# An attention loop over four chunks of time, with the norm and K product of the next chunk moved ahead of the recurrence and output product of this one

## What is computed

```python
x = x + attn(_layernorm(x))
# attn: xx is x shifted by one position
xk = x * time_mix_k + xx * (1.0 - time_mix_k)
xv = x * time_mix_v + xx * (1.0 - time_mix_v)
xr = x * time_mix_r + xx * (1.0 - time_mix_r)
k = xk @ W_key.T; v = xv @ W_value.T; r = xr @ W_receptance.T
sr = sigmoid(r)
# per channel, over t:  y = (p + e^(u+k) v) / (q + e^(u+k));
#   p = e^w p + e^k v;  q = e^w q + e^k      (w = -exp(time_decay), u = time_first)
out = (sr * y) @ W_output.T
```

## Time and profile before

| | us |
|---|---|
| median of the runs (2932.19 and 2935.12) | 2933.66 |
| the profiled execution, its own time | 2935.05 |
| span of its slowest core, first to last instruction | 2933.5 |
| span of its fastest core | 2923.3 |

### The profile page before, as it was taken

How to read it: one execution, slowest core, us unless ns; L and a number is a source line. 1 busy time by engine, 2 the same in 40 slices (tenths; PEclk the granted TensorE clock), 3 DMA queues, 4 the chain that set the end, 5 groups by cost and what they waited for, 6 DMA issues and landing times.

```text
span 2933.5 us, 21628 instructions; the slowest of 8 cores (2923.3 to 2933.5 us)
## 1 busy us (share of the span) xinstructions
PE 1877.2 (64%) x7648; PEld 785.1 (27%) x7648; DVE 1278.5 (44%) x1772; ACT 326.9 (11%) x551; POOL 67.9 (2%) x88
## 2 busy tenths in 40 slices
PE   3414324324322368878878878878878878888785
PEld 1101101101100123333333333333333333333332
DVE  5456456446455562143433423434434424424433
ACT  0320320210310000000000000010010010010000
POOL 0000000000001000000000000000000000000000
PEclk7757756656655689989989889989889889889897
DMA  6503503403209010021321321321311212213203
GB/s 149 81 0 69 75 0 51 64 0 55 31 0 129 1 24 1 1 36 15 50 36 15 51 36 15 51 36 15 50 24 28 38 27 37 36 17 49 29 1 115
DMA packets 69195, 112.79 MB, mean 38 GB/s; under 512 B 2480, under 2 KB 37312, under 8 KB 68048
## 3 DMA queue, kind: packets, MB, share of 16 engines
q0 software_dynamic: 63856, 94.50, 22.6%
q1 hardware_dynamic: 5232, 16.91, 1.8%
HBM read 197.28 MB, written 8.52 MB: 70 GB/s over the span
## 4 chain that ended last, share of the span: by engine, by line
PE 51%; DVE 9%; issue 2%; ACT 1%; DVEq 0%; DMA 0%; ACTq 0%; POOLq 0%
PE pc L638 18%; PE pc L664 15%; PE pc L652 14%; DVE h L707 4%; DVE sg L706 4%; PE pc L603 2%; PE pc L622 1%; ACT sg L736 1%; PE pc L611 1%; DVE h L677 1%; DVE acc L680 1%; DVE acc L715 0%; DVE h L689 0%; DVEq L36 0%; DMA cb<-comb_dram 0%
## 5 line engine op out<-in xcount | busy, mean ns | idle before, releaser
L638 PE MATMUL pc<-ln2x,wsl 128*128 128x512 bf16 x1920 | 521.6, 439 | 190.9 <-ACT sg L736 189.9
L664 PE MATMUL pc<-h,wsl 128*128 128x512 bf16 x1920 | 461.4, 404 | 101.6 <-DVE h L707 100.6
L706 DVE TENSOR_TENSOR sg<-sg,pc 128x512 f32<-128x512 f32 x240 | 164.9, 687 | 824.6 <-PE pc L652 805.2
L652 PE MATMUL pc<-ln2x,wsl 128*128 128x512 bf16 x1920 | 427.6, 379 | 0.0
L715 DVE TENSOR_TENSOR acc<-acc,pc 128x512 f32<-128x512 f32 x480 | 330.0, 688 | 183.5 <-PE pc L664 144.4
L638 PEld LDWEIGHTS pc<-ln2x,wsl 128*128 128x128 bf16 x1920 | 206.7, 110 | 504.6 <-issue 345.0
L736 ACT ACTIVATE sg<-pc 128x512 f32<-128x512 f32 x240 | 143.3, 597 | 1524.9 <-PE pc L638 1018.4
L338 PE MATMUL pb<-sry,wsla 128*128 128x512 bf16 x256 | 67.8, 435 | 379.7 <-DVE sry L257 379.7
L664 PEld LDWEIGHTS pc<-h,wsl 128*128 128x128 bf16 x1920 | 190.2, 102 | 372.8 <-issue 192.5
L652 PEld LDWEIGHTS pc<-ln2x,wsl 128*128 128x128 bf16 x1920 | 187.6, 98 | 230.2
L338 PE MATMUL pb<-mx,wsla 128*128 128x512 bf16 x512 | 127.3, 415 | 126.6 <-DVE mx L218 100.3
(11 more groups left out here) (118 smaller groups left out, 903.5 us busy)
## 6 DMA issues: line engine op xcount, KB each, us to landing
wsl<-gw POOLq DMA_DIRECT2D x15, 1024.0 KB, 11.5
wsl<-uw POOLq DMA_DIRECT2D x15, 1024.0 KB, 11.2
wsl<-dw POOLq DMA_DIRECT2D x15, 1024.0 KB, 12.0
acc<-x SPq DMA_DIRECT2D x4, 2048.0 KB, 24.4
wsla<-wk POOLq DMA_DIRECT2D x4, 2048.0 KB, 17.5
wsla<-wv POOLq DMA_DIRECT2D x4, 2048.0 KB, 19.0
wsla<-wr POOLq DMA_DIRECT2D x4, 2048.0 KB, 17.3
wsla<-wo POOLq DMA_DIRECT2D x4, 2048.0 KB, 17.7
```

What stands on the lines that cost most here:

```text
L638: inst = t.matmul(pc4[tc][:], slot_ap(3 * e)[:, kc, ocI * 128:(ocI + 1) * 128], ln2x[:, kc, 2 + tc * 512: 2 + (tc + 1) * 512], start=(kc = ...
L652: inst = t.matmul(pc4[4 + tc][:], slot_ap(3 * e + 1)[:, kc, ocI * 128:(ocI + 1) * 128], ln2x[:, kc, 2 + tc * 512: 2 + (tc + 1) * 512], sta ...
L664: inst = t.matmul(pc4[(oc % 2) * 4 + tc][:], slot_ap(3 * e + 2)[:, kcI, oc * 128:(oc + 1) * 128], h[:, kcI, tc * 512:(tc + 1) * 512], star ...
L706: VS.do(lambda sl=sl, tc=tc: v.tensor_tensor(sl[:], sl[:], pc4[4 + tc][:], OP.mult))
```

## The change

The norm, the difference and the K and V mixes of a chunk become a function `prework`. It is called once for chunk 0 ahead of the loop, and then for chunk `s_ + 1` inside chunk `s_`, between the evacuation of V and the recurrence. The statistics and the K product of chunk `s_ + 1` go with it: on TensorE they stand between R and O of chunk `s_`. O of chunk `s_` is added to `acc` in chunk `s_ + 1`, between the R mix and the evacuation of V. ScalarE makes the reciprocal root of chunk `s_ + 1` after the sigmoid of chunk `s_`. GpSimd's and SyncE's programs are not changed. No instruction is added or left out on any engine.

The diff, cut (the body of `prework` is the old code with `sp` for `s_`):

```diff
 @blk.vector
-                for s_ in range(NSC):
...
+                def prework(sp):
...
                     VS.do(lambda: v.tensor_tensor(xsq[:], ln1x[:, :, 1:], ln1x[:, :, 0:SCW], OP.subtract))
+                    if sp >= 1:
+                        v.wait_ge(s_pe, MS(f"t:MAT{4 * (sp - 1) + 2}"))
...
+                prework(0)
+                for s_ in range(NSC):
                     v.wait_ge(s_pe, MS(f"t:MAT{4 * s_ + 0}"))
+                    if s_ >= 1:
+                        v.wait_ge(s_sc, MS(f"s:ea{s_ - 1}_3"))
...
                     VS.ms[f"v:mixr{s_}"] = VS.v
+                    if s_ >= 1:
+                        psl = slice((s_ - 1) * SCW, s_ * SCW)
+                        v.wait_ge(s_pe, MS(f"t:MAT{4 * (s_ - 1) + 3}"))
+                        for od in range(CC):
+                            VS.do(lambda od=od, psl=psl: v.tensor_tensor(
+                                acc[:, od, psl], acc[:, od, psl], pb[od][:], OP.add))
+                        VS.ms[f"v:accev{s_ - 1}"] = VS.v
                     v.wait_ge(s_pe, MS(f"t:MAT{4 * s_ + 1}"))
...
                     VS.ms[f"v:vevac{s_}"] = VS.v
+                    if s_ + 1 < NSC:
+                        prework(s_ + 1)
                     for l in range(4):
...
 @blk.scalar
+                emit_rstd(0)
                 for s_ in range(NSC):
-                    s.wait_ge(s_dv, MS(f"v:var1_{s_}"))
-                    SS.do(lambda: s.activation(pb[2][:], pb[2][:], AF.Ln))
-                    SS.do(lambda: s.activation(pb[2][:], pb[2][:], AF.Exp, scale=-0.5), f"rstd1_{s_}")
                     emit_ea(s_, 0)
...
                     SS.ms[f"s:sig{s_}"] = SS.v
+                    if s_ + 1 < NSC:
+                        emit_rstd(s_ + 1)
                     emit_rden(s_, 0)
...
 @blk.tensor
+                def emit_stats(sp):
+                    t.wait_ge(s_dv, MS(f"v:xsq{sp}"))
+                    if sp >= 1:
+                        t.wait_ge(s_sc, MS(f"s:sigread_{sp - 1}"))
...
+                for s_ in range(NSC):
+                    m = 4 * s_ + 1
...
+                    t.wait_ge(s_dv, MS(f"v:kevac{s_}"))
                     if s_ >= 1:
                         t.wait_ge(s_dv, MS(f"v:accev{s_ - 1}"))
+                    emit_mat(m, mxb)
+                    m = 4 * s_ + 2
...
+                    emit_mat(m, mx)
+                    if s_ + 1 < NSC:
+                        emit_stats(s_ + 1)
+                        m = 4 * (s_ + 1)
...
+                        emit_mat(m, mx)
+                    m = 4 * s_ + 3
...
+                    if s_ + 1 < NSC:
+                        t.wait_ge(s_dv, MS(f"v:kevac{s_ + 1}"))
+                    emit_mat(m, sry)
```

More of the change, by code:

```diff
@@ L192, in _ @@
                 VS.do(lambda: v.memset(ones_b[:], 1.0), "setup")
-                for s_ in range(NSC):
[L194 to L200, removed]
+                def prework(sp):
+                    ssl = slice(sp * SCW, (sp + 1) * SCW)
+                    if sp >= 1:
+                        v.wait_ge(s_pe, MS(f"t:SQ1_{sp - 1}"))
+                    v.wait_ge(s_dx2[sp % 2], 16 * (sp // 2 + 1))
+                    VS.do(lambda ssl=ssl: v.tensor_copy(xb[:], acc[:, :, ssl]), f"xb{sp}")
+                    VS.do(lambda: v.tensor_tensor(xsq[:], xb[:], xb[:], OP.mult), f"xsq{sp}")
+                    v.wait_ge(s_pe, MS(f"t:SQ1_{sp}"))
                     VS.do(lambda: v.tensor_scalar_mul(m1_sb[:], pb[0][:], 1.0 / C))
@@ L203, in _ @@
                     VS.do(lambda: v.scalar_tensor_tensor(pb[2][:], pb[1][:], 1.0 / C, tA[:], OP.mult, OP.subtract))
-                    VS.do(lambda: v.tensor_scalar_add(pb[2][:], pb[2][:], EPS), f"var1_{s_}")
-                    v.wait_ge(s_sc, MS(f"s:rstd1_{s_}"))
-                    if s_ >= 1:
+                    VS.do(lambda: v.tensor_scalar_add(pb[2][:], pb[2][:], EPS), f"var1_{sp}")
+                    v.wait_ge(s_sc, MS(f"s:rstd1_{sp}"))
+                    if sp >= 1:
                         VS.do(lambda: v.tensor_copy(ln1x[:, :, 0:1], ln1x[:, :, SCW:SCW + 1]))
                     for l in range(4):
-                        lsl = slice(s_ * SCW + l * L, s_ * SCW + (l + 1) * L)
+                        lsl = slice(sp * SCW + l * L, sp * SCW + (l + 1) * L)
                         mbc = m1_sb[:, l * L:(l + 1) * L].unsqueeze(1).broadcast_to([128, CC, L])
@@ L214, in _ @@
                             ln1x[:, :, 1 + l * L:1 + (l + 1) * L], w1[:], rbc, OP.mult))
-                    VS.ms[f"v:ln1_{s_}"] = VS.v
+                    VS.ms[f"v:ln1_{sp}"] = VS.v
                     VS.do(lambda: v.tensor_tensor(xsq[:], ln1x[:, :, 1:], ln1x[:, :, 0:SCW], OP.subtract))
+                    if sp >= 1:
+                        v.wait_ge(s_pe, MS(f"t:MAT{4 * (sp - 1) + 2}"))
                     for cc in range(CC):
@@ L219, in _ @@
                             mx[:, cc, :], xsq[:, cc, :], TMK(cc), ln1x[:, cc, 0:SCW], OP.mult, OP.add))
-                    VS.ms[f"v:mixk{s_}"] = VS.v
+                    VS.ms[f"v:mixk{sp}"] = VS.v
                     for cc in range(CC):
@@ L223, in _ @@
                             mxb[:, cc, :], xsq[:, cc, :], TMV(cc), ln1x[:, cc, 0:SCW], OP.mult, OP.add))
-                    VS.ms[f"v:mixv{s_}"] = VS.v
+                    VS.ms[f"v:mixv{sp}"] = VS.v
+                prework(0)
+                for s_ in range(NSC):
+                    ssl = slice(s_ * SCW, (s_ + 1) * SCW)
                     v.wait_ge(s_pe, MS(f"t:MAT{4 * s_ + 0}"))
+                    if s_ >= 1:
+                        v.wait_ge(s_sc, MS(f"s:ea{s_ - 1}_3"))
                     for od in range(CC):
@@ L258, in _ @@
                             sry[:, :, ksl], srl[:, :, ksl], w1[:], OP.mult), f"sry{s_}_{l}")
[L259 to L263, removed]
+                sN = NSC - 1
+                v.wait_ge(s_pe, MS(f"t:MAT{4 * sN + 3}"))
+                for od in range(CC):
+                    VS.do(lambda od=od: v.tensor_tensor(
+                        acc[:, od, sN * SCW:(sN + 1) * SCW],
+                        acc[:, od, sN * SCW:(sN + 1) * SCW], pb[od][:], OP.add))
+                VS.ms[f"v:accev{sN}"] = VS.v
             @blk.scalar
@@ L271, in _, with emit_rstd @@
                 SS.do(lambda: s.activation(ew[:], ew[:], AF.Exp), "ew2")
+                def emit_rstd(sp):
+                    s.wait_ge(s_dv, MS(f"v:var1_{sp}"))
+                    SS.do(lambda: s.activation(pb[2][:], pb[2][:], AF.Ln))
+                    SS.do(lambda: s.activation(pb[2][:], pb[2][:], AF.Exp, scale=-0.5), f"rstd1_{sp}")
                 def emit_ea(s_, l):
@@ L310, in _ @@
                 t.wait_ge(s_dv, MS("v:setup"))
+                def emit_stats(sp):
+                    t.wait_ge(s_dv, MS(f"v:xsq{sp}"))
+                    if sp >= 1:
+                        t.wait_ge(s_sc, MS(f"s:sigread_{sp - 1}"))
+                    for cc in range(CC):
+                        inst = t.matmul(pb[0][:], ones_b[:], xb[:, cc, :], start=(cc == 0), stop=(cc == CC - 1))
+                    TS_.mark(inst, f"S1_{sp}")
+                    for cc in range(CC):
+                        inst = t.matmul(pb[1][:], ones_b[:], xsq[:, cc, :], start=(cc == 0), stop=(cc == CC - 1))
+                    TS_.mark(inst, f"SQ1_{sp}")
@@ new lines, in emit_mat @@
+                def emit_mat(m, rhs_t):
+                    for od in range(CC):
+                        for kc in range(CC):
+                            inst = t.matmul(pb[od][:],
+                                            wsl_a[m % 2][:, kc, od * 128:(od + 1) * 128],
+                                            rhs_t[:, kc, :],
+                                            start=(kc == 0), stop=(kc == CC - 1))
+                    TS_.mark(inst, f"MAT{m}")
+                emit_stats(0)
+                t.wait_ge(s_dwa, 16)
@@ L311, in _ @@
+                t.wait_ge(s_dv, MS("v:mixk0"))
+                emit_mat(0, mx)
                 for s_ in range(NSC):
-                    t.wait_ge(s_dv, MS(f"v:xsq{s_}"))
+                    m = 4 * s_ + 1
+                    t.wait_ge(s_dwa if m % 2 == 0 else s_dwb, 16 * (m // 2 + 1))
+                    t.wait_ge(s_dv, MS(f"v:mixv{s_}"))
+                    t.wait_ge(s_dv, MS(f"v:kevac{s_}"))
                     if s_ >= 1:
                         t.wait_ge(s_dv, MS(f"v:accev{s_ - 1}"))
-                    for cc in range(CC):
-                        inst = t.matmul(pb[0][:], ones_b[:], xb[:, cc, :], start=(cc == 0), stop=(cc == CC - 1))
@@ L317, in _ @@
[L317 to L322, removed]
-                        t.wait_ge(s_dwa if m % 2 == 0 else s_dwb, 16 * (m // 2 + 1))
[L324 to L342, removed]
@@ new lines, in _ @@
+                    emit_mat(m, mxb)
+                    m = 4 * s_ + 2
+                    t.wait_ge(s_dwa if m % 2 == 0 else s_dwb, 16 * (m // 2 + 1))
+                    t.wait_ge(s_dv, MS(f"v:mixr{s_}"))
+                    t.wait_ge(s_dv, MS(f"v:vevac{s_}"))
```

(14 more changed lines are left out.)

## The result

The changed kernel takes 2962.45 us (median of seven runs), the kernel before 2932.32 (six runs). So the change costs 29.1 us, a ratio of 1.0098, 95% interval 1.0084 to 1.0112; forecast were 32.5 us and 2966.

The account below looks back on a forecast made before the run. VectorE's single serial row of work and waits was taken to bound the attention: 218.4 us of waits come, 185.9 go, net +32.5 us on 2933.66, so 2966 us, 1.1% slower; range 2945 to 2992.

Parts of the forecast that it names:

- What goes: VectorE's waits that vanish over three chunk boundaries (O, statistics, K, V, first reciprocals): 185.9 us in total.
- 14.4 us that stay: At line 256, twelve reciprocal waits keep 1.2 us each; 56.0 of their 70.4 us go.
- O before the add: VectorE's add of O into acc waits for O, which starts after K's evacuation: 10.6 us a boundary.
- V's evacuation: VectorE waits because V's weight load is held until O is done, then V runs: 28.5 us a boundary.
- The mean: Next chunk's statistics wait for R and ScalarE's sigmoid, covered only by cast and square: 33.7 us a boundary.
- The sum: New waits of 72.8 us a boundary, 218.4 for three, less 185.9 that go: net +32.5 us.
- Not slower, V's weights no wait: Rival at TensorE between O and V: load hidden beneath the add, 34.5 us less, 2932; chance 4%.
- Evenly shared loads: Rival: V's and R's loads share the engines, V's weights up to 17.5 us later, 52 more, 3018; chance 6%.
- The second part: Rival behind the attention: TensorE's granted clock shifts its time, expected no more than 10 us; chance it decides 4%.

Follow-up runs that it names:

- the reordered loads: Changed kernel with weight loads issued, and slots alternating, in the order the products run, so V's load waits for the K product: 2935.3 us, ratio 0.9982.
- the half quarter put back: Changed kernel with the first half of the recurrence's first quarter done between the next chunk's square and mean: 2925.3 us, ratio 0.9935.
- the wait for two tiles: Changed kernel with the statistics waiting only until ScalarE has read the two PSUM tiles they overwrite, the variance until the third: 2937.2 us, ratio 0.9984.
- the second group of experiments: Three runs on another chip: changed kernel again (2963.0 us), statistics behind two tiles (2937.2), all three edits (2863.5); kernel before 2940.9.
- the two groups of experiments: Four experiments on one chip, then three on another; the kernel before, timed again in each, stood at 2944.2 and 2940.9 us.

## Why the prediction was right

**What goes** was right: K's wait is gone, and the first reciprocal's too. Its 14.4 us that stay were about 15: 38.5 less the last chunk's 20.0 is 18.5 for 15 waits, 1.23 each.

**O before the add**: forecast 10.6 a boundary, measured 28.7 / 3 = 9.6. O took 16.67, 15.71 and 15.87 us, where I had taken 17.1.

**V's evacuation**: forecast 28.5, measured 28.6. The mechanism is right, but that the size fits to 0.1 us is luck: V started 19.5 us behind O and not 18.0, and V itself took 15.4 us and not 16.7, so two terms were off and cancel. The 17.5 us of the load was moreover one core's: in the kernel before, the same load, alone, took 14.9 to 17.9 us over the eight cores. That the load is the cause is shown by the reordered loads: with the dependence gone the wait is 16.9, all of it V.

**The mean**: forecast 33.7, measured 33.5. That it is the cover that was lost is shown by the half quarter put back (20.5), and that R's sigmoid is what stands in between, by the wait for two tiles (21.0).

**The sum**: 28.7 + 85.8 + 100.4 = 214.9 came, 218.4 were forecast. The attention as a whole grew by 30.4, not 32.5, and the part behind it shrank by 2.4: 28.0 between the two profiles, 29.1 between the medians. The closeness of the total is in part luck too. The rows of one core gave the forecast, while the attention grew by 18.5 to 37.2 us from core to core, and in the second group of experiments the two kernels lay 22 us apart.

**The rivals.** Not slower, V's weights no wait: out, as V started 19 us behind O with the DMA as releaser. Its price was 34.5 us; taking the wait away gave 27.7, since the price took products to be of one length and they were 9.4 us longer in all. Evenly shared loads: out; V's landed after 18.8 and R's after 28.9 us, one behind the other. The Trainium skill ("DMA: Bandwidth & Descriptors", section "Two DMAs through the same engine are not ordered") says that descriptors of one queue start in order but are pipelined, and that nothing orders DMAs across the 16 engines. If V's later landing comes from that, which no run here shows, its effect is small: 0.6 to 1.4 us of 17.4. The second part changed by 2.4 us between the slowest cores and by at most 9.9 on one core, under the 10 allowed.

## What to carry to other kernels

When work is hoisted out of one place, ask what it stood between: the distance may have been what hid a weight load or let another engine finish. Buffers that alternate by the number of the product, and not by the order in which products run, put two users of one slot next to each other as soon as the order changes. Wait for the buffers that are overwritten and not for the whole set: two tiles of eight were 25.8 us here. Where one engine holds all work in one row, a ledger of its waits (those that go, those that come, with what covers each) gives the change to a few microseconds.

## What the runs showed of the hardware

Of two loads of 2 MB in one GpSimd queue, issued 0.87 us apart, the first landed 18.8 us after its issue and the second 28.9; alone a load took 17.4. So the second landed 11 us behind the first, less than the 17.4 of a load by itself. These are slowest cores. The same pair took 13.6 and 24.4 us at one boundary on core 0 of the same run: how fast a load lands differs by core, and from run to run (on core 0 V started 15.0 us behind O in this run of the changed kernel and 19.2 in its later one). As the metric is the slowest core, a load that is waited for counts at its slowest.

TensorE's granted clock in a product begins at half (1.2 GHz: 0.50 to 0.66 over the first 4 us after an idle stretch) and goes to full (2.4 GHz, 1.00). In some products it is at 0.81 for a part or for all of the rest, and the same 64 matmuls take up to 18.3 us and not 15.3. The kernel before had this too: O at 640.51 took 18.27, at 0.81 after its first 4 us. It made the gain of the reordered loads about 9 us smaller. Which products it hits differed between the variants, and no run here was made to tell why. The Trainium skill ("TensorE: Matmul & The Clock Gate", "Seeing it yourself") tells of a current limiter that takes a whole die to 13/16 once three of its cores run dense matmuls; the value agrees with the 0.81 of the windows. Whether three cores were busy at once, no run here shows, since each core's times count from its own start. From 318 to 326 us of their own times cores 6 and 7 had 0.81 with the reordered loads, and cores 4 and 5 of the same die 1.00.

Open too is why the kernel before took 12 and 9 us longer in the two groups of experiments and the changed one did not. Its slowest core was granted 0.798 to 0.803 of the clock there, but for one run at 0.790, and 0.804 in the first profile, which goes with it and doesn't explain it.
